# A graph layer with a mixture of experts on one core: one-hots made tile by tile, one of them made earlier, bias products with 128 rows

## What is computed

```python
def _rgcn_conv(x, edge_index, edge_type, basis, comp, root, bias):
    W = jnp.einsum('rb,bde->rde', comp, basis)
    h = jnp.einsum('nd,rde->nre', x, W)
    msg = h[src, edge_type]
    seg = dst * R + edge_type
    sums = jax.ops.segment_sum(msg, seg, num_segments=n * R)
    cnt = jax.ops.segment_sum(jnp.ones(...), seg, num_segments=n * R)
    mean = sums / jnp.maximum(cnt, 1.0)[:, None]
    return mean.reshape(n, R, -1).sum(axis=1) + x @ root + bias
...
h = relu(_rgcn_conv(layernorm(x), ...)); h = relu(_rgcn_conv(h, ...))
x = x + take(h @ lin_w, node_type) + lin_b[node_type]
xn = layernorm(layernorm(x)) * gamma + beta
logits = xn @ Wr + br                      # top 2 of 8, softmax over the two: w_full
for e in range(8):
    y += (gelu(xn @ W1[e] + b1[e]) @ W2[e] + b2[e]) * w_full[..., e, None]
return x + y
```

## Time and profile before

| | |
|---|---|
| median of 3 runs | 4807.63 us (4806.77 to 4810.96) |
| the profiled execution | 4807.05 us, its span 4805.2 us |
| busy in the span | PE 3782.7 us (79%), PEld 3282.0 (68%), DVE 3014.4 (63%), ACT 880.3 (18%), POOL 3332.3 (69%) |
| first layer | about 190 to 2390 us, 49 pairs |
| second layer | about 2390 to 4805 us, 49 pairs |
| mean granted TensorE clock | 0.79 of full speed |

### The profile page before, as it was taken

One profiled execution on the slowest core, in us unless ns is written; L12 is line 12 of the kernel. 1 busy time (PEld: TensorE's weight loads), 2 busy tenths in 40 slices (PEclk: granted clock), 3 DMA queues, 4 the chain that ended last, 5 costly groups with the idle time before them and its releaser, 6 DMA issues.

```text
span 4805.2 us, 119647 instructions
## 1 busy us (share of the span) xinstructions
PE 3782.7 (79%) x38119; PEld 3282.0 (68%) x38120; DVE 3014.4 (63%) x6579; ACT 880.3 (18%) x2470; POOL 3332.3 (69%) x3374
## 2 busy tenths in 40 slices
PE   1366666666666666666559999999999999999999
PEld 1255555555555555555448888888888888888888
DVE  4556656766666676666446676767666666666663
ACT  2200000000000000000003333333333333333333
POOL 0477777777777777777477777777777777676770
PEclk9555555555555555555569999999999999999999
DMA  4656655555555555555456555555555555555550
GB/s 128 194 172 183 176 158 156 158 158 157 156 158 158 155 159 157 156 157 159 115 168 168 160 160 160 157 161 156 160 159 162 157 160 161 157 161 157 162 160 21
DMA packets 344661, 749.10 MB, mean 156 GB/s; under 512 B 128323, under 2 KB 167806, under 8 KB 344430
## 3 DMA queue, kind: packets, MB, share of 16 engines
q0 software_dynamic: 215040, 662.09, 49.0%
q1 hardware_dynamic: 115510, 70.49, 5.6%
q10 hardware_dynamic: 14076, 16.04, 1.0%
HBM read 719.00 MB, written 29.35 MB: 156 GB/s over the span
## 4 chain that ended last, share of the span: by engine, by line
PE 43%; DVE 24%; issue 15%; DMA 9%; POOL 8%; DVEq 1%; SPq 0%; ACT 0%; POOLq 0%; ACTq 0%
DVE mixed L913 11%; POOL slot L558 8%; PE bank L1251 8%; PE bank L1338 8%; PE bank L1283 8%; PE bank L1351 8%; DMA slot<-table,idx 7%; DVE inv L939 4%; PE bank L1247 3%; DVE scaled L945 3%; PE bank L1311 2%; PE bank L1312 2%; DVE o L1024 2%; PE bank L1279 1%; DVE inv L938 1%
## 5 line engine op out<-in xcount | busy, mean ns | idle before, releaser
L558 POOL DMA_INDIRECT slot<-table,idx x3354 | 3326.6, 992 | 1308.2 <-issue 1045.0
L1251 PE MATMUL bank<-hot,slot 128*128 (+1 forms) x21168 | 1240.9, 211 | 63.2 <-DMA slot<-table,idx 54.6
L1251 PEld LDWEIGHTS bank<-hot,slot 128*128 128x128 bf16 x21168 | 994.4, 108 | 125.6 <-issue 69.2
L1247 PE MATMUL bank<-hot,ones_b 128*128 x1764 | 398.7, 226 | 744.9 <-DMA slot<-table,idx 337.8
L1247 PEld LDWEIGHTS bank<-hot,ones_b 128*128 128x128 bf16 x1764 | 180.9, 103 | 1007.1 <-issue 969.3
L1338 PE MATMUL bank<-xnT,ffn_w 128*128 128x128 f32 x6272 | 791.4, 279 | 49.2 <-DVE scaled L945 49.1
L1338 PEld LDWEIGHTS bank<-xnT,ffn_w 128*128 128x128 f32 x6272 | 740.7, 192 | 80.7 <-DVE scaled L945 58.3
L1351 PE MATMUL bank<-ffn_w,act 128*128 128x256 f32 x3136 | 761.6, 386 | 0.3 <-DVE o L1024 0.2
L1351 PEld LDWEIGHTS bank<-ffn_w,act 128*128 128x128 f32 x3136 | 565.5, 190 | 78.0 <-issue 16.9
L913 DVE SCALAR_TENSOR_TENSOR mixed<-scaled,small,mixed 128x256 f32<-128x256 f32 x1372 | 573.7, 481 | 12.2
L913 DVE SCALAR_TENSOR_TENSOR mixed<-scaled,comp_sb,mixed 128x256 f32<-128x256 f32 x1372 | 573.5, 481 | 10.5
(11 more groups left out here) (148 smaller groups left out, 2189.0 us busy)
## 6 DMA issues: line engine op xcount, KB each, us to landing
slot<-table,idx POOLq DMA_INDIRECT x3354
inv<-inv_d SPq DMA_DIRECT2D x98, 256.0 KB, 3.7
table<-ffn_w SPq DMA_DIRECT2D x7, 1344.0 KB, 6.0
table<-parts ACTq DMA_DIRECT2D x49, 192.0 KB, 3.2
ffn_w<-in_L_ffn_W_dram SPq DMA_DIRECT2D x16, 512.0 KB
xcur<-in_x_dram SPq DMA_DIRECT2D x48, 128.0 KB
out_dram<-o ACTq DMA_DIRECT2D x48, 128.0 KB
ffn_w<-in_x_dram SPq DMA_DIRECT2D x6, 896.0 KB, 8.9
```

Of the source, the lines that this page charges most:

```text
L558: gp.indirect_dma_start(out=slot[:, k, :], out_offset=None, in_=table[layer], in_offset=bass.IndirectOffsetOnAxis(ap=idx[:, h, k:k + 1], a ...
L1247: t.matmul(C[:, at], ones_b[:, :], oh, start=(k == 0), stop=(k == TILES - 1), skip_group_check=True)
L1251: last = t.matmul(S[f][:, at], slot[:, k, q * D + f * P:q * D + (f + 1) * P], oh, start=(k == 0 and q == 0), stop=(k == TILES - 1 and q == ...
```

## The change

`one_hots_fast` compared all 18 tiles in one VectorE instruction with two inputs (`tensor_tensor`, 1152 columns). Now it issues 18 instructions with one tensor input and a scalar per partition (`tensor_scalar`, 64 columns each); only the last one signals. In the second layer `one_hots(1, x)`, with the short memset in front of it, moves from behind the last mixing and `expert(r, 6)` to behind `expert(r, 5)`, still ahead of `scale(1, 0, x)`. `tmaskT`, `linb_sb`, `wfT` and `b2_sb` have 128 partitions, the unused ones zero (four memsets by GpSimd at the start), so that the two bias products use all rows. The router's bias is loaded into all partitions and added by VectorE while it reads the logits; its product is gone.

```diff
-        linb_sb = sb("linb_sb", [TYPES, D], F32)
-        b2_sb = sb("b2_sb", [EXPERTS, D], F32)
-        br_sb = sb("br_sb", [1, EXPERTS], F32)
+        linb_sb = sb("linb_sb", [P, D], F32)
+        b2_sb = sb("b2_sb", [P, D], F32)
+        br_sb = sb("br_sb", [P, EXPERTS], F32)
...
+            sp.wait_ge(s_const, 3)
+            sp.dma_start(linb_sb[0:TYPES, :], lin_b).then_inc(weights_in, 16)
+            sp.dma_start(b2_sb[0:EXPERTS, :], b2).then_inc(weights_in, 16)
+            sp.dma_start(br_sb[:, :], br.partition_broadcast(P)).then_inc(weights_in, 16)
...
+            for z in (linb_sb, b2_sb, tmaskT, wfT):
+                gp.memset(z[:, :], 0.0)
...
-                v.tensor_tensor(hot[:, h, :, :], iota_b[:, :].unsqueeze(1).broadcast_to([P, TILES, COLS]),
-                                rel[:, h, :].unsqueeze(2).broadcast_to([P, TILES, COLS]),
-                                ALU.is_equal).then_inc(hot_ready, 1)
+                for k in range(TILES):
+                    last = v.tensor_scalar(hot[:, h, k, :], iota_b[:, :], rel[:, h, k:k + 1], None, ALU.is_equal)
+                last.then_inc(hot_ready, 1)
...
-                v.tensor_copy(lg[:, :], LG).then_inc(lg_read, 1)
+                v.tensor_tensor(lg[:, :], LG, br_sb[:, :], ALU.add).then_inc(lg_read, 1)
...
+                        if e == 5 and x is not None:
+                            plain(3)
+                            one_hots(1, x + PAIRS)
                     if x is not None:
-                        plain(3)
-                        one_hots(1, x + PAIRS)
                         scale(1, 0, x + PAIRS, x)
...
                 for k in range(HALVES):
-                    t.matmul(LG, xnext[:, k, :], wr_sb[:, k, :], start=(k == 0), stop=False)
-                t.matmul(LG, ones_f[0:1, :], br_sb[:, :], start=False, stop=True).then_inc(lg_done, 1)
+                    last = t.matmul(LG, xnext[:, k, :], wr_sb[:, k, :], start=(k == 0), stop=(k == HALVES - 1))
+                last.then_inc(lg_done, 1)
```

More of the change, by code:

```diff
@@ L129, in build @@
         tmask = sb("tmask", [P, TYPES], F32)
-        tmaskT = sb("tmaskT", [TYPES, P], F32)
+        tmaskT = sb("tmaskT", [P, P], F32)
         x1 = sb("x1", [P, D], F32)
@@ L145, in build @@
         wfull = sb("wfull", [P, 3, EXPERTS], F32)
-        wfT = sb("wfT", [EXPERTS, P], F32)
+        wfT = sb("wfT", [P, P], F32)
         act = sb("act", [P, 2, HCH, P], F32)
@@ L379, in _ @@
                              b1.rearrange("e (c p) -> p e c", p=P)).then_inc(weights_in, 16)
-            sp.dma_start(linb_sb[:, :], lin_b).then_inc(weights_in, 16)
-            sp.dma_start(b2_sb[:, :], b2).then_inc(weights_in, 16)
-            sp.dma_start(br_sb[:, :], br.rearrange("(a e) -> a e", a=1)).then_inc(weights_in, 16)
+            sp.wait_ge(s_const, 3)
+            sp.dma_start(linb_sb[0:TYPES, :], lin_b).then_inc(weights_in, 16)
+            sp.dma_start(b2_sb[0:EXPERTS, :], b2).then_inc(weights_in, 16)
+            sp.dma_start(br_sb[:, :], br.partition_broadcast(P)).then_inc(weights_in, 16)
             sp.dma_start(wr_sb[:, :, :], Wr.rearrange("(k p) e -> p k e", p=P)).then_inc(weights_in, 16)
@@ L728, in dense @@
                     act_.wait_ge(wfT_ps, r + 1)
-                    sc.activation(wfT[:, :], T2[0:EXPERTS, 256:256 + P], ACT.Copy).then_inc(wfT_done, 1)
+                    sc.activation(wfT[0:EXPERTS, :], T2[0:EXPERTS, 256:256 + P], ACT.Copy).then_inc(wfT_done, 1)
                     gelu(r, 7)
@@ L978, in masks @@
                 v.tensor_scalar(tmask[:, :], iota8[:, 0:TYPES], ntcol[:, 0:1], None, ALU.is_equal)
-                v.tensor_scalar(tmaskT[:, :], ntrow[:, :], pid[0:TYPES, 0:1], None,
+                v.tensor_scalar(tmaskT[0:TYPES, :], ntrow[:, :], pid[0:TYPES, 0:1], None,
                                 ALU.is_equal).then_inc(mask_done, 1)
```

## The result

The changed kernel takes 4901.26 us (median of 4 runs, 4890.95 to 4904.86) against 4807.2 us for the kernel before in the same comparison: the ratio is 1.0192 (95% interval 1.0174 to 1.0209). The profiled execution took 4890.95 us, its span is 4888.9 us.

The account below looks back on a forecast made before the run. GpSimd's gathers pace the first layer; in the second, TensorE's stretch to the logits plus VectorE's to the end of `scale`. 4807 + 46 x (1.36 + 1.36) = +125, -63 - 4: 4865 us, range 4785 to 4935.

Parts of the forecast that it names:

- the likeliest case: Rival (1): first layer's gathers faster, second layer longer with a falling clock; 4830 to 4900 us, likeliest 4865, chance 0.50.
- first layer, total: First layer: two long gathers per pair lose their cause, 1.30 us per pair over 48 pairs, 63 us gained.
- wider products, router's bias: Second layer: router's bias product gone, -0.31 us, and bias product with full rows, -0.30 us per pair.
- the open wait before `scale`: Second layer, VectorE: wait formerly hidden under the one-hots now follows `expert(r, 6)`'s addition openly, +0.22 us per pair.
- the series: Second layer, VectorE: 18 one-hot instructions at 0.15 us each take 2.70 us instead of 1.28, +1.42 us per pair.
- gathers that hold the series: Second layer, VectorE: the series meets two gathers, each holding it about 0.16 us, +0.33 us per pair.
- the clock: Second layer, TensorE: wait of 3.6 us lowers the clock for 3 us per pair, costing +1.36 us; bounds 0 and 3.1.
- the ends of the second layer: Second layer's first two pairs, still paced by gathers, and last pairs with lighter bias products: together 4 us gained.
- Rival (3): Second layer: instruction starts 0.07 us apart, series 1.3 us, clock holds, total 4723 us; chance 0.10.
- rival (5): Second layer: series of 0.20 us per instruction, or clock low for 6.83 us each pair; 4940 to 4960 us, chance 0.10.
- the cover of about 6 us: First layer, TensorE's block 1: 6 us of cover absorbs the one-hots' extra 1.8 us, so their delay costs nothing.
- Rival (4): First layer gains nothing, as gapless short instructions hold gathers like one long one; total 4928 us, chance 0.08.

Follow-up runs that it names:

- tiles_first_layer: Changed kernel, but the second layer's one-hots in one two-input instruction again, at their new place; first layer keeps the 18: 4725.7 us, ratio 0.9832.
- one_instruction: Changed kernel with the old single two-input one-hot instruction in both layers; the move and the bias products stay: 4788.37 us, ratio 0.9962.
- bias_only_again: Changed kernel with one one-hot instruction in both layers at the old place, repeating bias_only, whose first try met a slower chip: 4778.21 us, ratio 0.9936.
- fill_the_wait: Changed kernel plus 44 unused bf16 products of 128 columns in front of TensorE's second-layer wait for `scaled`: 4791.21 us, ratio 0.9969.
- long_one_input: tiles_first_layer plus an unused 2048-column one-input instruction behind each first-layer series: 5997.84 us on a slower chip where the kernel before takes 5938.84 us.
- two_inputs_18: tiles_first_layer with the first layer's 18 instructions given two SBUF inputs: 6018.18 us on a slower chip where the kernel before takes 5938.84 us.
- third_buffer_18: Changed kernel with a third one-hot buffer, block 1's one-hots made at the top of the turn, 18 instructions in both layers: 4662.3 us, ratio 0.9697.
- hots_only: Kernel before with the 18 instructions alone in both layers, no move, bias products as before: 4851.29 us, ratio 1.0094.

## Why the prediction was right

The direction and the likeliest case (the first layer faster, the second slower, with a falling clock) came out; 4901 us is 36 us above the 4865 and just over the 4900 that I gave as the upper end of that case. By the steps, in us per pair of the second layer:

| step | predicted | measured, and from where |
|---|---|---|
| first layer, total | -63 | -62.7, tiles_first_layer against one_instruction |
| wider products, router's bias | -0.61 | -0.62, bias_only_again 46.81 against 47.43 |
| the open wait before `scale` | +0.22 | +0.26, one_instruction 47.07 against 46.81 |
| the series | +1.42 | +1.43, fill_the_wait 48.50 against 47.07 |
| gathers that hold the series | +0.33 | 0, as +1.43 is the whole cost of the series |
| the clock | +1.36 | +2.33, 50.83 against 48.50 |

Together 1.07 + 2.33 = 3.40 us; 46 of them are 156 us, and 4807 + 156 - 62 = 4901. In part the total came near by luck: the clock was taken 0.97 us per pair too low (45 us in all) and the holds 0.33 too high (15 us). For the 4 us that I gave for the ends of the second layer no run has a row of its own.

**The series.** The starts are 0.149 us apart (over the series of the second layer the 18th starts 2.54 us after the first), as L978's 0.13 us had announced: an instruction with a scalar per partition from SBUF does not reach the 0.07 us of L1008. Rival (3) needed a series under 1.6 us. That makes 18 x 0.149 = 2.7 us, as in the sum. The holds lengthen single instructions of a series, to as much as 0.50 us from a median of 0.23, but not the next start: behind instructions of over 0.35 us it comes 0.146 us later, behind those of up to 0.26 us 0.147 us later. So the term for them should not have stood there.

**The clock** is the term that was mis-sized: I took 3 us of low clock per pair, and it was 5.7 us on average. Most turns have 6.83, for 51.20 - 48.50 = 2.70 us, 40% of it (the bound of the forecast had 45%, 3.1 us). The reason that I gave for taking less, that TensorE is full on both sides of the wait, did not count: it was just as full, and the clock still stayed low for as long as at 2487 us. The bound named in rival (5), low for 6.83 us each pair, is what happened in most turns. The total stayed under that rival's 4940 us since the clock cost 2.33 us per turn and not 3.1 (35 us), and the other terms were smaller by 0.29 us (13 us). The other half of rival (5) was summed wrongly: a series of 0.20 us per instruction adds 0.9 us per pair, which makes 4906 us and not 4940.

**The logits.** The loop as I described it (from the logits on) needs a correction. VectorE no longer waits for the logits; its unbroken stretch begins at the product of expert 2 (3019.78, with 0.19 us of idle time ahead), so a part of what the router's product saved need not be on the path in the changed kernel; how much, no run shows. The total of the bias changes was still right in the kernel where it was tested.

**The first layer** gained what two lengthened gathers had cost, and the cover of about 6 us hid the longer series, as predicted. The reason was only half right. I read the hold as one of two SBUF inputs until the instruction's end; long_one_input shows that a long instruction with one input holds gathers too, and two_inputs_18 that short ones with two inputs mostly do. What the change found is the one form of the four tried that holds nothing: short, with one input. Rival (4) fell by the trace of the changed kernel. The Trainium skill (SBUF — State Buffer, who interferes with whom) says more than I quoted from it: a VectorE instruction with two SBUF inputs contends with a GpSimd instruction that reads SBUF, and a `tensor_scalar` in a two-port mode takes the whole shared pair. My reading of it here is that the first delays only a gather that has yet to read its indices, and the second also one that is already under way. The 0.44 us and the 0.57 us cases above fit that, but do not show it. The same section of the Trainium skill also says that whichever of the two engines issues first has the pair for its whole instruction; here the trace differs, as the gather that began 0.57 us ahead of the long instruction was held all the same (1.90 us). Why 64-column instructions, which the same rule would let into that mode, hold nothing, no run here shows.

## What to carry to other kernels

Before an instruction is made longer to spare another engine, find out on whose stretch it stands: the same 18 instructions gained 63 us where VectorE had 15 us to spare, cost 1.43 us per turn where it set the end, and cost nothing once they stood in its idle time (third_buffer_18). A longer wait of TensorE is not paid once: here 2.1 us more of it cost 2.33 us per turn by the lower clock, more than the 1.07 us by which the turn itself had grown, and useless products put into the wait gave that back. Split a change by layer and try the halves: with the wider bias products in both kernels, the good half alone was worth 1.7%, and together with the second layer's one-hots moved to a slack place it was worth 3.0%.

## What the runs showed of the hardware that was not expected

- By the wait of TensorE per turn, with full work around it: at 0.75 (fill_the_wait), 1.07 (the kernel before), 1.45 (bias_only_again) and 1.75 us (tiles_first_layer, one_instruction) the granted clock stayed at 1.00 over thousands of us (but for one stretch of 3.41 us in each of the last two), at 2.46 us (hots_only) it fell in about every second turn for 3.41 us, at 3.2 us (the changed kernel) in nearly every turn, mostly for 6.83 us. 3.41 us of low clock made a turn 1.6 us longer in both of these kernels.
- A gather that starts 0.07 us after the first of eight mixing instructions is held as well. In the changed kernel, second layer, POOL and DVE:

```profile
2987.57 2.42 POOL L561 DMA_INDIRECT slot<-table,idx  x1 [0.30 <-PE bank L1255]
```

```profile
2984.83 2.77 DVE L933 TENSOR_SCALAR hot<-iota_b,rel 128x64 bf16<-128x64 bf16 x18 [0.33 <-issue]
2987.50 3.38 DVE L916 SCALAR_TENSOR_TENSOR mixed<-scaled,comp_sb,mixed 128x256 f32<-128x256 f32 x8
```

It ends at 2989.99. The fourth of the eight instructions ends at 2989.17, 0.82 us before that. 37 gathers in 2000 us of the second layer were held so, by 55 us in all. TensorE's only wait there is the one for `scaled`, so it did not wait for them. The prediction had said of such a stream in the first layer that it delays a gather by little, and there it is so: no gather of the changed kernel takes over 1.04 us.
